# A block of attention and feed-forward layers: another order of TensorE's work, a third value buffer, and the last stage's probability blocks in the k blocks' buffer

## The chip, the cores and the metric

One NeuronCore of a Trainium2 chip. Times are device microseconds of one execution of the program; smaller is better. TensorE (PE) multiplies matrices, VectorE (DVE), ScalarE (ACT) and GpSimd (POOL) work on elements, and SyncE (SP) starts transfers. Each runs its own list of instructions in order and waits on semaphores. SBUF is the memory next to the engines; PSUM, in banks, takes TensorE's results.

## The reference, cut to what matters

x has 32 sequences of 32 positions and 512 channels. Attention has 32 heads of 16.

```python
def attn(x, wq, wk, wv, wo):                 # x here is cond(x): a 32x32 matrix for each sequence
    q, k, v = proj(wq), proj(wk), proj(wv)   # [B, head, T, 16]
    q, k = rope(q), rope(k)
    scores = where(causal, q @ k.T / 4, -inf)
    return (softmax(scores) @ v).merge_heads() @ wo.T

def cond2(x):                                # a linear layer, and LoRA experts, two of eight per token
    gates = top2_softmax(x @ Wr.T + 5 * onehot(language))
    return x @ W.T + 2 * einsum(x @ A, gates, B)

x = x + attn(cond(x, weights[subject]), ...)
x = x + unperm(gelu(perm(cond2(x)) @ up) @ down)    # 16 small feed-forward blocks
```

## The kernel before

The 1024 tokens are 8 tiles of 128; two tiles (t = 0, 1) make a stage's group, and the stages are g = 0 to G-1 = 3. Products of fp32 weights are three matmuls of a high and a low fp32r part (`mm3`); ScalarE writes the high part of every operand (`cond_hi`, `o_out`, `x1_out`) and VectorE the low part (`cond_lo`, `o_lo`, `x1_lo`).

The order of each engine's work is written out by hand in a loop over g. In stage g TensorE does, interleaved: the scores of group g; the feed-forward of group g-1 (`lora_down`, `experts_base`, `turn_logits`, `turn_gates`, `experts_lora`, `ffn_up`, `ffn_down`); the projections of group g+1 (`qk`, `v`); the products of probabilities and values of group g (`pv(g, t, c)`, four chunks c for a tile); and last the output projection `wo_proj(g)`, which needs the high and low parts of both tiles' outputs. `cond` of group g+1 stands at the head of stage g (for g = 1, 2). After the loop comes the feed-forward of group 3 alone, and the scattered output.

The probabilities' way in a stage: `max_shift` (VectorE, from PSUM: maximum and difference) -> `exp` (ScalarE) -> `sums` (VectorE: sum and reciprocal) -> `norm` (GpSimd) -> `turn` (VectorE: transposes of 32x32) -> `probs_block(g, t, i)` (ScalarE): four copies of 32 partitions x 512 that put each sequence's probabilities in its place of the block-diagonal buffer `pbd[:, i]`, the rest of which is zero. `pbd` has two halves i and serves both tiles, so a tile's copy waits for the products that read the half before. k too is laid out in blocks (`kbd`, `k_blocks` on VectorE and GpSimd, after `rope`). `v_out` (ScalarE) copies the values into `vz[:, t]`, one buffer for each tile of a group, when the last group's products of that tile are done; it stands ahead of `o_out` for the same tile. `attn` is the same memory as `xc`, which `cond_hi` and `cond_lo` fill.

PSUM's banks are three rings: A (2 banks: cond, q, k, v; in the last stage pv too), S (2: scores, `ffn_down`) and F (4: pv, `wo_proj`, the rest). The n-th item of a ring takes bank n modulo its size and waits until the item before it in that bank has been read.

The gates of the experts are a chain of small operations on VectorE (`gates_top`, `gate_exp` on ScalarE, `gates_out`, then `turn_gates` on TensorE and `gate_h`), and `experts_lora` waits for it. ScalarE then changes its table (`gelu_table`), copies `x2_out`, and does eight `gelu`s in two halves, each between `ffn_up` and `ffn_down`.

Lines of the page: L504 to L506 are `mm3`, L531 `cond`, L569 and L578 scores, L596 `pv`, L676 `ffn_up`, L688 `ffn_down`, L802 all plain copies of ScalarE, L884 `gelu`, L1005 low parts from PSUM, L1068 and L433 k blocks, L1088 and L1090 `sums`, L1096 `turn`, L418 and L422 GpSimd's part of `rope`, L391 and L479 the memsets of `pbd`, L394 and L401 gathers, L1183 the gathers' indices `idx`, L1030 `blocks`, from which `cond` of group 0 takes its matrices, L1120 and L1140 the logits' copy and the first step of `gates_top`, L1167 the last of `gates_out`, L1176 a cast in `gate_h`, L853 `gelu_table`.

## Time and profile before

| | |
|---|---|
| median of 3 runs | 252.77 us (252.18 to 253.22) |
| the profiled execution: its time, its span | 251.96 us, 250.2 us |
| busy: TensorE, VectorE, ScalarE, GpSimd | 205.5, 147.8, 119.0, 120.0 us |
| mean granted clock of TensorE | 0.952 of full speed |
| stages 0, 1, 2 (start of the stage's work on TensorE) | 39.7, 72.3, 123.9 us |
| stage 3, its `wo_proj` | 175.2, 212.7 us |
| last product of TensorE ends | 239.4 us |

The span runs from the first to the last instruction of the profiled execution; its own time is a little longer. "Busy" is time in which the engine worked; a wait is shown as idle time ahead of an instruction, with the instruction that ended it. The granted clock is 1.0 at 2.4 GHz and 0.5 at 1.2 GHz.

### The profile page before, as it was taken

The numbers are of one execution on the slowest core, as the hardware profiler recorded it, in microseconds if no ns is written. First come the engines' busy times: TensorE is split into PE (matmuls) and PEld (weight loads), VectorE is DVE, ScalarE is ACT, GpSimd is POOL, SyncE is SP. The second block draws the span as 40 slices with busy tenths as digits, with TensorE's granted clock in tenths as the row PEclk, the third lists the DMA queues.
The fourth block names the chain that finished last, engine by engine and source line by source line (L and its number), as shares of the span: only waits on it lengthen the run. The fifth ranks groups of instructions, "written<-read, shape, count | busy, mean of one in ns | idle before, by whom it ended". The sixth has DMA issues, their size and how long they took to land.

```text
span 250.2 us, 5702 instructions
## 1 busy us (share of the span) xinstructions
PE 205.5 (82%) x2404; PEld 176.3 (70%) x2404; DVE 147.8 (59%) x309; ACT 119.0 (48%) x199; POOL 120.0 (48%) x94
## 2 busy tenths in 40 slices
PE   0579997999699999995999999949994828987910
PEld 0579956997598999674988997739883615976500
DVE  3547999968757979681377794832688402235000
ACT  3271537744232238793161379651515995133720
POOL 8258959788700059698200396983003322500054
PEclk9999999999999999998899999998998895999995
DMA  7799823000013000003341000024200003320024
GB/s 235 213 358 344 282 64 107 3 0 3 1 48 125 0 3 3 3 3 42 42 128 45 3 0 0 3 27 59 88 3 0 1 0 45 45 84 0 3 25 59
DMA packets 11273, 15.60 MB, mean 62 GB/s; under 512 B 2320, under 2 KB 7088, under 8 KB 11248
## 3 DMA queue, kind: packets, MB, share of 16 engines
q1 hardware_dynamic: 8224, 11.65, 14.0%
q0 software_dynamic: 2736, 3.57, 9.3%
q8 instruction: 19, 0.31, 0.5%
q10 hardware_dynamic: 288, 0.01, 0.1%
q14 instruction: 6, 0.05, 0.1%
HBM read 10.91 MB, written 4.33 MB: 61 GB/s over the span
## 4 chain that ended last, share of the span: by engine, by line
PE 60%; DVE 14%; ACT 12%; issue 7%; POOL 2%; DMA 2%; POOLq 1%; ACTq 0%; DVEq 0%
PE ps_F L504 8%; PE ps_A L504 8%; PE ps_F L506 7%; PE ps_F L505 7%; PE ps_A L506 7%; PE ps_A L505 7%; ACT pbd L802 7%; PE ps_F L596 3%; PE ps_F L676 3%; PE ps_A L531 3%; PE ps_S L578 2%; ACT act L884 2%; POOL out L453 2%; ACT xc L802 2%; DVE xc L1005 2%
## 5 line engine op out<-in xcount | busy, mean ns | idle before, releaser
L461 POOL TENSOR_TENSOR pr<-pr,small 128x512 f32<-128x512 f32 x16 | 16.5, 1046 | 66.3 <-DVE small L1090 66.3
L802 ACT ACTIVATE pbd<-pr 32x512 f32<-32x512 f32 x64 | 40.2, 628 | 9.8 <-DVE pr L1096 5.0
L453 POOL DMA_INDIRECT out<-y,row_at x16 | 25.1, 1571 | 39.8 <-ACT y L802 36.1
L504 PE MATMUL ps_F<-xc,woT 128*128 128x256 f32 x64 | 19.7, 307 | 6.1 <-DVE xc L1005 6.1
L433 POOL TENSOR_TENSOR kbd<-kr,cst 128x512 f32<-128x512 f32 x16 | 20.7, 1318 | 2.7 <-PE ps_F L513 2.6
L418 POOL TENSOR_TENSOR rot<-rot,cst 128x512 f32<-128x512 f32 x14 | 18.1, 1292 | 7.7 <-DVE rot L1046 7.7
L1068 DVE TENSOR_TENSOR kbd<-kr,cst 128x512 f32<-128x512 f32 x16 | 19.9, 1280 | 2.4 <-POOL kr L422 2.4
L504 PE MATMUL ps_A<-xc,wqT 128*128 128x256 f32 x64 | 18.9, 296 | 2.7 <-DVE xc L1005 2.7
L505 PE MATMUL ps_F<-xc,woT 128*128 128x256 f32 x64 | 19.2, 300 | 0.0
L506 PE MATMUL ps_F<-xc,woT 128*128 128x256 f32 x64 | 19.1, 299 | 0.0
L802 ACT ACTIVATE x<-xt 128x512 fp32r<-128x512 f32 x8 | 5.0, 631 | 28.9 <-DVE xt L1108 28.9
L504 PEld LDWEIGHTS ps_F<-xc,woT 128*128 128x128 f32 x64 | 13.5, 212 | 7.5 <-issue 7.5
L506 PE MATMUL ps_A<-xc,wqT 128*128 128x256 f32 x64 | 18.6, 290 | 0.0
L505 PE MATMUL ps_A<-xc,wqT 128*128 128x256 f32 x64 | 18.5, 289 | 0.0
L504 PE MATMUL ps_A<-xc,wkT 128*128 128x256 f32 x64 | 18.3, 286 | 0.0
L504 PE MATMUL ps_F<-x,w2T 128*128 128x256 f32 x64 | 18.3, 286 | 0.0
L884 ACT ACTIVATE act<-ps_F 128x512 f32<-128x512 f32 x32 | 16.5, 604 | 3.4 <-PE ps_F L676 3.3
L506 PE MATMUL ps_A<-xc,wkT 128*128 128x256 f32 x64 | 17.9, 279 | 0.0
L505 PE MATMUL ps_A<-xc,wkT 128*128 128x256 f32 x64 | 17.9, 279 | 0.0
L506 PE MATMUL ps_F<-x,w2T 128*128 128x256 f32 x64 | 17.8, 279 | 0.0
L505 PE MATMUL ps_F<-x,w2T 128*128 128x256 f32 x64 | 17.8, 279 | 0.0
L531 PE MATMUL ps_A<-wbd,xs 128*128 128x128 f32 x64 | 9.7, 315 | 9.1 <-DVE wbd L1030 9.1
(149 smaller groups left out, 606.0 us busy)
## 6 DMA issues: line engine op xcount, KB each, us to landing
xs<-in_x SPq DMA_DIRECT2D x4, 512.0 KB, 6.4
xt<-in_xT SPq DMA_DIRECT2D x4, 512.0 KB, 3.5
out<-xt SPq DMA_DIRECT2D x4, 512.0 KB, 3.7
pbd<-in_L_attn_wq SPq DMA_DIRECT2D x2, 512.0 KB, 4.7
act<-in_L_attn_wk SPq DMA_DIRECT2D x1, 1024.0 KB, 5.5
act<-in_L_attn_wv SPq DMA_DIRECT2D x1, 1024.0 KB, 8.2
act<-in_L_attn_wo SPq DMA_DIRECT2D x1, 1024.0 KB, 8.2
x<-in_L_cond_A SPq DMA_DIRECT2D x1, 256.0 KB, 9.8
```

The costliest lines, as they stand in the source:

```text
L418: pool.tensor_tensor(rv, rv, con("sin").unsqueeze(1).to_broadcast([P, 2 * N // T, T]), ALU.mult).then_inc(rot_sin, 1)
L433: pool.tensor_tensor(kbd[:, t, c, :, :].rearrange("p b (h s) -> p b h s", h=HG), kv.unsqueeze(2).to_broadcast([P, BT, HG, T]), con("head") ...
L453: pool.indirect_dma_start(out=out, out_offset=bass.IndirectOffsetOnAxis(ap=row_at[:, g, c:c + 1], axis=0), in_=y[:, c, :], in_offset=None, ...
L461: pool.tensor_tensor(pr[:, i, :, :], pr[:, i, :, :], mx[:, i, :].unsqueeze(2).to_broadcast([P, NH // 2, T]), ALU.mult).then_inc(normed, 1)
L504: pe.matmul(dst, hi_l, hi_r, start=start, stop=False, skip_group_check=skip)
L505: pe.matmul(dst, hi_l, lo_r, start=False, stop=False, skip_group_check=skip)
L506: return pe.matmul(dst, lo_l, hi_r, start=False, stop=stop, skip_group_check=skip)
L531: last = pe.matmul(bank(it)[:, P * c:P * c + P], xs[:, g % XS, t, P * c:P * c + P], wbd[:, t, :, :], start=True, stop=True)
L596: last = pe.matmul(bank(it)[32 * j:32 * j + 32, P * c:P * c + P], vz[:, t, 4 * c + j, HD * e:HD * e + 2 * HD], pbd[:, c // 2, HC * (c % 2) ...
L802: return sc.activation(dst, src, ACT.Copy)
L884: sc.activation(act[:, r, j, :, :], bank(it)[:, :].rearrange("p (h n) -> p h n", h=2), ACT.Gelu).then_inc(s_free(it), 1)
L1068: ve.tensor_tensor(kbd[:, t, c, :, :].rearrange("p b (h s) -> p b h s", h=HG), kv.unsqueeze(2).to_broadcast([P, BT, HG, T]), con("head").u ...
```

## The change

1. `cond(g+2)` of stages 0 and 1 stands ahead of `wo_proj(g)`, in place of the head of stage g+1; its copies `cond_hi` and `cond_lo` stand between and behind `x1_out` and `x1_lo`. As `attn` is `xc`, `cond_hi` waits for the whole of `wo_proj`.
2. In stages 1 and 2 tile 0's products come in pairs after each `ffn_up`, and tile 1's around `ffn_down`'s second half.
3. pv moves from the F (and A) ring to the S ring.
4. `vz` has three buffers in turn, and `v_out` waits for the product three tiles back. It now stands ahead of y_out, and `o_out(g, 1)` behind both.
5. In the last stage tile 0's blocks are made before exp 2 and 3 and its products come right behind `turn_gates`; tile 1's blocks go into the two halves of `kbd`, which GpSimd first zeroes (`kbd_zeros`); two of each block's four copies are VectorE's (`probs_half`).
6. The memset of `pbd[:, 1]` on GpSimd stands behind the three first gathers.

```diff
-        vz = sb("vz", [P, GT, NH // 2, 3 * HD])
+        vz = sb("vz", [P, 3, NH // 2, 3 * HD])
+        def pbd_of(g, t, i):
+            return kbd_pbd[i] if (g, t) == (G - 1, 1) else pbd[:, i, :, :, :]
+        def S_at(g):
+            return 8 * g - 2 if g else 0
         def S_scores(g, i):
-            return "S", 4 * g + 2 * max(0, g - 1) + i
+            return "S", S_at(g) + i
+        def PVi(g, t):
+            return "S", S_at(g) + 4 + (2 if g else 1) * t
         def S_down(g, h):
-            return "S", 4 * min(g + 2, G) + 2 * g + h
+            return "S", S_at(g + 1) + (5 + 2 * h if g + 1 < G else h)
...
             pool.memset(vz[:, :, :, :], 0.0).then_inc(vz_zero, 1)
-            pool.memset(pbd[:, 1, :, :, :], 0.0).then_inc(pbd_zero, 1)
...
+            def kbd_zeros(t):
+                wait_full(pool, S_scores(G - 1, 2 * t + 1))
+                pool.memset(kbd[:, t, :, :, :], 0.0).then_inc(kbd_zero, 1)
...
             cond_seqs()
+            pool.memset(pbd[:, 1, :, :, :], 0.0).then_inc(pbd_zero, 1)
```

On TensorE, the head and the middle of stages 1 and 2, and the middle of stage 3:

```diff
-                    if more:
-                        cond(g + 1, 0)
-                        cond(g + 1, 1)
                     scores(g, 0)
...
                 if more:
                     qk(g + 1, "wq", Q, 1)
+                else:
+                    for c in range(KC):
+                        pv(g, 0, c)
...
                     qk(g + 1, "wk", K_, 0)
                     ffn_up(g - 1, 0)
+                    pv(g, 0, 0)
+                    pv(g, 0, 1)
                     qk(g + 1, "wk", K_, 1)
                     ffn_up(g - 1, 1)
+                    pv(g, 0, 2)
+                    pv(g, 0, 3)
+                    v(g + 1, 0)
                     ffn_down(g - 1, 0)
                     ffn_down(g - 1, 1)
-                    v(g + 1, 0)
-                    for c in range(KC):
-                        pv(g, 0, c)
+                    v(g + 1, 1)
+                    pv(g, 1, 0)
+                    pv(g, 1, 1)
                     ffn_down(g - 1, 2)
                     ffn_down(g - 1, 3)
-                    v(g + 1, 1)
-                    for c in range(KC):
-                        pv(g, 1, c)
+                    pv(g, 1, 2)
+                    pv(g, 1, 3)
...
                     ffn_up(g - 1, 0)
-                    pv(g, 0, 0)
-                    pv(g, 0, 1)
                     ffn_up(g - 1, 1)
+                    pv(g, 1, 0)
+                    pv(g, 1, 1)
                     ffn_down(g - 1, 0)
                     ffn_down(g - 1, 1)
-                    pv(g, 0, 2)
-                    pv(g, 0, 3)
-                    for c in range(KC):
-                        pv(g, 1, c)
+                    pv(g, 1, 2)
+                    pv(g, 1, 3)
                     ffn_down(g - 1, 2)
                     ffn_down(g - 1, 3)
+                if g + 2 < G:
+                    cond(g + 2, 0)
+                    cond(g + 2, 1)
                 wo_proj(g, 0)
                 wo_proj(g, 1)
```

ScalarE's and then VectorE's order in stage 3 after the change (several calls to a line here):

```python
exp(g, 0); h_out(g - 1); exp(g, 1); gate_exp(g - 1)
probs_block(g, 0, 0); probs_block(g, 0, 1)
exp(g, 2); exp(g, 3); o_out(g, 0)
gelu_table(g - 1); x2_out(g - 1); gelu(g - 1, 0)
probs_block(g, 1, 0); probs_block(g, 1, 1)
gelu(g - 1, 1); o_out(g, 1); y_out(g - 1, 0); y_out(g - 1, 1)

max_shift(g, 0); max_shift(g, 1); logits_out(g - 1)
sums(g, 0); sums(g, 1); gates_top(g - 1)
turn(g, 0); turn(g, 1); max_shift(g, 2); gates_out(g - 1)
probs_half(0, 0); probs_half(0, 1); max_shift(g, 3); gate_h(g - 1)
sums(g, 2); sums(g, 3); o_lo(g, 0); turn(g, 2); turn(g, 3)
probs_half(1, 0); probs_half(1, 1); o_lo(g, 1)
```

The new helper on VectorE:

```diff
+            def probs_half(t, i):
+                ve.wait_ge(turned, 4 * (G - 1) + 2 * t + i + 1)
+                if t:
+                    ve.wait_ge(kbd_zero, i + 1)
+                else:
+                    wait_pv(ve, 8 * (G - 1) + 2 * i - 3)
+                for b in range(2, BT):
+                    at = slice(T * b, T * b + T)
+                    last = ve.tensor_copy(pbd_of(G - 1, t, i)[at, :, b, :], pT(2 * t + i)[at, :, :])
+                last.then_inc(pbd_v, 1)
```

## Rows read from the trace of the kernel before

**Rows 1.** The page's fourth part: the chain that ended last, by engine.
```profile
PE 60%; DVE 14%; ACT 12%; issue 7%; POOL 2%; DMA 2%; POOLq 1%; ACTq 0%; DVEq 0%
```

**Rows 2.** Stretches of the span: busy time of each engine, granted clock, DMA.
```profile
core 0: us, PE busy (x) PEld busy (x) DVE busy (x) ACT busy (x) POOL busy (x), PEclk, DMA share, GB/s
72.30:74.10 1.80, 1.80 (x19) 1.79 (x18) 0.91 (x2) 0.88 (x2) 0.00 (x0) 1.00 0.00 0
112.40:116.60 4.20, 1.08 (x32) 0.81 (x32) 0.98 (x2) 2.18 (x4) 3.73 (x3) 1.00 0.28 31
116.60:120.00 3.40, 3.34 (x16) 3.37 (x17) 0.00 (x0) 0.00 (x0) 2.79 (x3) 0.51 0.65 70
175.20:187.70 12.50, 12.50 (x210) 10.55 (x208) 9.79 (x31) 4.33 (x7) 0.00 (x0) 1.00 0.14 45
202.00:206.10 4.10, 0.00 (x1) 0.00 (x0) 0.00 (x0) 4.02 (x8) 1.58 (x1) 0.92 0.00 0
206.10:209.20 3.10, 1.93 (x32) 1.51 (x32) 0.69 (x1) 3.04 (x5) 1.56 (x1) 0.50 0.75 84
```

**Rows 3.** TensorE's timeline: start, us, line, operation; [idle before, and who ended it].
```profile
66.57 0.35 PE L504 MATMUL ps_F<-xc,woT 128*128 128x256 f32 x1 [2.02 <-DVE xc L1005]
...
116.66 0.53 PE L504 MATMUL ps_F<-xc,woT 128*128 128x256 f32 x1 [2.02 <-DVE xc L1005]
...
190.91 0.39 PE L504 MATMUL ps_F<-hg,bT 128*128 128x256 f32 x1 [3.16 <-DVE hg L1178]
```

**Rows 4.** GpSimd's and VectorE's timelines at the start, two rows of each.
```profile
2.06 1.80 POOL L391 MEMSET pbd<- 128x2048 f32 x1
...
6.89 1.03 POOL L401 DMA_INDIRECT kr<-in_L_cond_weights,ids  x1 [0.30 <-issue]
...
3.15 0.74 DVE L1183 TENSOR_SCALAR idx<-ids,cst 128x8 uint32<-128x8 int32 x1 [3.15 <-DMA cst<-constants]
...
8.21 0.74 DVE L1030 TENSOR_SCALAR wbd<-wg,cst 128x64 f32<-128x64 f32 x4 [1.03 <-DMA wg<-in_L_cond_weights,idx]
```

**Rows 5.** VectorE, GpSimd and ScalarE at the end of stage 1's attention.
```profile
105.06 1.45 DVE L1068 TENSOR_TENSOR kbd<-kr,cst 128x512 f32<-128x512 f32 x1
...
106.04 1.61 POOL L422 TENSOR_TENSOR kr<-kr,rot 128x512 f32<-128x512 f32 x1
...
114.70 0.60 ACT L802 ACTIVATE vz<-ps_A 128x512 f32<-128x512 f32 x1 [1.20 <-PE ps_F L596]
115.20 0.59 ACT L802 ACTIVATE xc<-ps_F 128x512 fp32r<-128x512 f32 x1
```

**Rows 6.** Groups of stage 3, 175.2 to 212.7: busy us, mean ns, idle before.
```profile
L802 ACT ACTIVATE pbd<-pr 32x512 f32<-32x512 f32 x16 | 10.0, 626 | 0.2
...
L676 PE MATMUL ps_F<-x,upw 32*128 32x256 f32 x32 | 4.6, 522 | 0.0
...
L884 ACT ACTIVATE act<-ps_F 128x512 f32<-128x512 f32 x8 | 4.1, 603 | 0.1
...
L1096 DVE STREAM_TRANSPOSE pr<-pr 128x512 f32<-128x512 f32 x4 | 2.8, 696 | 1.2 <-POOL pr L461 1.2
...
L688 PE MATMUL ps_S<-act,dn 128*32 128x256 f32 x32 | 2.7, 473 | 0.0
...
L1088 DVE TENSOR_REDUCE small<-pr 128x16 f32<-128x512 f32 x4 | 2.6, 656 | 0.0
...
L853 ACT ACT_TABLE_LOAD x1 | 1.3, 1283 | 0.0
...
L1090 DVE RECIPROCAL small<-small 128x16 f32<-128x16 f32 x4 | 1.0, 253 | 0.1
```

**Rows 7.** VectorE's timeline in stage 3, three rows around the gates.
```profile
181.51 0.17 DVE L1140 TENSOR_TENSOR small<-ps_F,small 128x16 f32<-128x16 f32 x1 [1.03 <-PE ps_F L635]
...
186.62 0.29 DVE L1167 TENSOR_SCALAR act<-small 128x256 f32<-128x256 f32 x1
...
189.43 0.96 DVE L1176 CAST hg<-act 128x256 fp32r<-128x256 f32 x1
```

More of the change, by code:

```diff
@@ L149, in ropes_to @@
             return 4 * g + i if g else min(i + 1, 3)
+        kbd_pbd = [kbd[:, i, :, :, :].rearrange("p c b k -> p (c b k)").rearrange("p (h b t) -> p h b t", b=BT, t=T)
+                   for i in range(2)]
+        def pbd_of(g, t, i):
+            return kbd_pbd[i] if (g, t) == (G - 1, 1) else pbd[:, i, :, :, :]
         def pT(i):
@@ L867, in probs_block @@
                     sc.wait_ge(pbd_zero, 2)
-                for b in range(BT):
+                for b in range(BT if g < G - 1 else 2):
                     at = slice(T * b, T * b + T)
-                    last = copy(pbd[at, i, :, b, :], pT(2 * t + i)[at, :, :])
+                    last = copy(pbd_of(g, t, i)[at, :, b, :], pT(2 * t + i)[at, :, :])
                 last.then_inc(pbd_a, 1)
@@ L945, in _ @@
                     gate_exp(g - 1)
-                else:
-                    probs_block(0, 0, 0)
-                    probs_block(0, 0, 1)
+                if g in (0, G - 1):
+                    probs_block(g, 0, 0)
+                    probs_block(g, 0, 1)
                 exp(g, 2)
                 exp(g, 3)
+                if not more:
+                    o_out(g, 0)
                 if g:
@@ L953, in _ @@
                     x2_out(g - 1)
[L954 to L955 removed]
+                if not more:
                     gelu(g - 1, 0)
[L957 removed]
+                    probs_block(g, 1, 0)
+                    probs_block(g, 1, 1)
                     gelu(g - 1, 1)
+                    o_out(g, 1)
                     y_out(g - 1, 0)
[L960 to L963 removed]
                     y_out(g - 1, 1)
[L965 removed]
+                else:
+                    if g:
+                        probs_block(g, 0, 0)
+                        gelu(g - 1, 0)
+                        probs_block(g, 0, 1)
+                        gelu(g - 1, 1)
+                    probs_block(g, 1, 0)
                     v_out(g + 1, 0)
                     o_out(g, 0)
[L968 to L971 removed]
+                    if g:
+                        y_out(g - 1, 0)
+                    probs_block(g, 1, 1)
                     v_out(g + 1, 1)
[L973 to L975 removed]
+                    if g:
+                        y_out(g - 1, 1)
+                    o_out(g, 1)
                 x1_out(g, 0)
+                if g + 2 < G:
+                    wait_full(sc, Fi(g, "WO", 1))
+                    cond_hi(g + 2, 0)
                 x1_out(g, 1)
+                if g + 2 < G:
+                    cond_hi(g + 2, 1)
             h_out(G - 1)
@@ L1221, in _ @@
                 more = g + 1 < G
-                if g:
-                    if more:
-                        cond_lo(g + 1, 0)
-                        cond_lo(g + 1, 1)
-                if g:
+                if g and not more:
+                    max_shift(g, 0)
+                    max_shift(g, 1)
+                    logits_out(g - 1)
+                    sums(g, 0)
+                    sums(g, 1)
+                    gates_top(g - 1)
+                    turn(g, 0)
+                    turn(g, 1)
+                    max_shift(g, 2)
+                    gates_out(g - 1)
+                    probs_half(0, 0)
+                    probs_half(0, 1)
+                    max_shift(g, 3)
+                    gate_h(g - 1)
+                    sums(g, 2)
+                    sums(g, 3)
+                    o_lo(g, 0)
+                elif g:
                     max_shift(g, 0)
@@ L1236, in _ @@
                     sums(g, 1)
-                    if more:
-                        rope(g + 1, 0)
+                    rope(g + 1, 0)
                     turn(g, 0)
@@ L1242, in _ @@
                     sums(g, 3)
-                    if more:
-                        rope(g + 1, 1)
+                    rope(g + 1, 1)
                 else:
@@ L1268, in _ @@
                     w_los("r", raw_r, rT, 1)
-                else:
+                elif more:
                     if g + 2 < G:
                         blocks(g + 2)
-                    if more:
-                        rope(g + 1, 2)
-                    if more:
-                        rope(g + 1, 3)
-                        for t in range(GT):
-                            k_blocks(g + 1, t, 0)
-                            k_blocks(g + 1, t, 2)
+                    rope(g + 1, 2)
+                    rope(g + 1, 3)
+                    k_blocks(g + 1, 0, 0)
+                    k_blocks(g + 1, 0, 2)
                     o_lo(g, 0)
+                    k_blocks(g + 1, 1, 0)
+                    k_blocks(g + 1, 1, 2)
                     o_lo(g, 1)
-                for i in range(2):
-                    add_x(g, i)
-                    x1_lo(g, i)
+                else:
+                    probs_half(1, 0)
+                    probs_half(1, 1)
+                    o_lo(g, 1)
+                add_x(g, 0)
+                x1_lo(g, 0)
+                add_x(g, 1)
+                if g + 2 < G:
+                    cond_lo(g + 2, 0)
+                x1_lo(g, 1)
+                if g + 2 < G:
+                    cond_lo(g + 2, 1)
             logits_out(G - 1)
```

55 lines of the change are left out of this document (22 added, 33 removed).

## The prediction

> **What bounds the kernel now.** I read the chain of waits first: three fifths of it is TensorE, the rest copies of ScalarE and VectorE and waits between engines [rows 1]. So I next cut TensorE's time into stretches, to find where it idles or runs slowly [rows 2], and then asked its timeline who ended each idle time [rows 3]. Four things show.
>
> First, the last copies of the attention output (ScalarE's high part, VectorE's low part) hold TensorE for 2.02 us ahead of `wo_proj` in stages 0 and 1 [rows 3]; stage 2 repeats this. Second, in stage 1 the clock pays as well: from 112.4 to 116.6 TensorE is busy for 1.08 of 4.20 us (the 2.02, and 1.16 for tile 1's last probabilities), and then the granted clock is 0.51, its 1.2 GHz level, until 120.0 [rows 2]. Stage 2 repeats this too. In stage 0 a gap of 2.02 alone stood behind dense work, and its first matmul took 0.35 us, against 0.53 in stage 1 [rows 3]: no fall. Third, `cond`, at the head of stages 1 and 2, takes 1.8 us of a full TensorE [rows 2]. Fourth, stage 3 (175.2 to 212.7, 37.5 us) is TensorE's only to 187.7: it is then held 3.16 us for the gates [rows 3], and afterwards ScalarE is the bound. From 202.0 to 206.1 ScalarE is busy for 4.02 us and TensorE for none, and the clock is 0.50 in the next stretch [rows 2]. ScalarE's largest group there is 16 copies of probabilities, 10.0 us [rows 6].
>
> **Stage 0 to 1: 2.0 us less.** `cond(2)` moves from stage 1's head, where nothing hides it, into the gap ahead of `wo_proj`, and its copies go to the stage's end. That takes 1.8 us off the head. The gap itself shrinks: `v_out` of tile 1 used to wait for the product `pv(g,1,3)` because it overwrote the same `vz`; with a third `vz` it goes ahead, and `o_out` starts 0.50 us sooner (vz at 114.70, xc at 115.20 [rows 5]). The chain of copies becomes 1.5 us, `cond` 1.8, so the longer stands: 2.02 - 1.8 = 0.2. The price is in the copies behind: ScalarE's wait for `wo_proj`'s second half delays only `cond_hi` and `x1_out(g,1)`, which needs that half anyway; VectorE's `x1_lo(g,1)` comes one copy (0.7) later, but `lora_down` needs it only 2.9 us behind the head. `max_shift` comes sooner, as one `cond_lo` no longer stands ahead of `x1_lo`. I cost this at nothing; without its cover it is 0.7 us per stage.
>
> **Stage 1: 4.6 less.** `pv(1,0,.)` moves ahead of `v(2,0)`, so pbd comes free some 8 us sooner, ScalarE fills tile 1's blocks earlier, and the wait of 1.16 goes. `cond(3)` again gives 1.8 + 0.2. Without the idle stretch the clock should stay up: 3.4 us at 0.51 held 1.7 us of work, so 1.6 goes. Against it, TensorE now reaches `turn_logits` just as VectorE has copied the logits: 0.15. Sum: 1.16 + 1.8 + 0.2 + 1.6 - 0.15 = 4.6.
>
> The new orders on the two S banks must not stall it. `pv(1,1,0)` needs the bank that `o_lo(1,0)` reads, and that copy stands on VectorE behind two k blocks, of which the second waits for GpSimd's last rope addition (106.04 + 1.61 [rows 5], 1.9 sooner here, so 105.75). With a k block of 1.45 [rows 5] and a copy of 0.7 the bank is free at 108.0. TensorE began tile 1's products 1.08 ahead of 112.4 [rows 2], so at 111.3; 1.9 sooner, and 1.0 for the `ffn_down` pair that now stands behind them, gives 108.4. The margin is 0.4 us.
>
> **Stage 2: 3.1 less.** As stage 1 without a `cond`: 1.16 + 0.5 + 1.6 - 0.15. One gap of 1.5 stays, as in stage 0, where the clock held.
>
> **Stage 3: 5.3 less (3.4 to 7.2).** Up to the gates' product at 190.9 it gets longer. Ahead of `gate_h` VectorE now has a second sum with reciprocal (0.66 + 0.25 [rows 6], and 0.1 of waiting), two transposes (2 x 0.70 [rows 6]) and `probs_half` for tile 0, four copies of 32x512. Such a copy isn't in this trace. From below: 256 elements in 0.29 and small operations in 0.17 [rows 7] give 0.17 + 2 x 0.12 = 0.42 us; from above 0.70, a transpose. I take 0.4, as it is the same kind of move between two tiles in SBUF, so 1.6 (up to 2.8). Back come VectorE's idle 1.03 ahead of the gates, which the sums fill, and 0.67 of the cast, which took 0.96 beside GpSimd [rows 7]. Net 0.9 + 0.1 + 1.4 + 1.6 - 1.03 - 0.67 = 2.3 later.
>
> The Trainium skill ("VectorE: DVE Perf Modes", Mode 2x_2P) says that a copy with one source and both ends in SBUF moves two fp32 elements a cycle, which would give 0.42 as well; by its plain mode it would be 0.7, and the sum 1.1 worse.
>
> From there to `wo_proj` it took 21.8 us (190.9 to 212.7). Now ScalarE has 8 copies of probabilities fewer, and the four of tile 0 lie in its earlier idle time; tile 1's no longer wait for tile 0's products, as they have their own buffer. Its chain: table load and lookup 1.5 [rows 6], `x2_out` 0.6, `ffn_up` to the first gelu 1.2 (my estimate: over half of a half's 2.3, of which half at the low clock [rows 6]), gelu 2.06 (four at a time overlap a little [rows 6]), four copies 2.5, gelu 2.06, `o_out` 0.6, `y_out` 0.6, `ffn_down` 1.07: 12.3. But TensorE now waits for much of the time around the gates, and with the clock at 1.2 GHz its own chain is longer: one pv pair takes 1.93 in place of 1.08 [rows 2], and `ffn_down`'s two pairs, one at either clock, 2.7 in all [rows 6], so 1.0 and 1.7. Then it is 1.5 + 0.6 + 1.8 + 2.06 + 1.26 = 7.2 up to the first block, 1.9 + 1.7 + 1.9 for pv, ffn_down, pv, then 0.6 + 0.6 + 1.7 and some 0.5 of hand-overs: 16.1. Behind the gates the work is denser, so part of it runs at full clock; I take the middle, 14.2. The stage gives 21.8 - 14.2 - 2.3 = 5.3. The new memsets of kbd (1.80 each, as [rows 4]) lie on GpSimd where it waits for sums.
>
> **The start: 1.0 more.** The memset of pbd's second half moves from ahead of the first gather to behind the third. At 2.06 it held VectorE's 8-column `idx` for 0.74 us, to 0.03 behind the memset's end [rows 4]. Without it the gathers start 0.55 sooner. But then the memset runs from 7.4 to 9.2, and `blocks(0)`, four scalar multiplications that took 0.74 at 8.21, right behind the third gather's end at 7.92 [rows 4], meets it: it ends at 9.95 in place of 8.95, and `cond`, the first product, waits for it. Ends: 0.55 less (no collision) and 1.3 more.
>
> The Trainium skill ("SBUF — State Buffer", Who interferes with whom) says that such one-source operations and GpSimd lock each other out of a shared port pair for a whole instruction, by who comes first; the trace agrees (0.96 for 0.29 [rows 7]), and by the rule the loss is this 1.0.
>
> **Sum.** The profiled execution took 251.96 us with a span of 250.2, 1.76 around it; the median of the runs shown is 0.81 higher, 252.77. Off come 2.0 + 4.6 + 3.1 + 5.3 - 1.0 = 14.0. Span 236.2, its execution 238.0, median 238.8 us. The tail behind `wo_proj(3)`, 37.5, has no edit.
>
> **Rivals.** *The clock is not won.* Idle time of only 1.5 to 1.8 still lets it fall in stages 1 and 2, and stage 3 goes at its slow end: 2 x 1.6 + 1.9 more, 243.9. For it: the fall behind the 4.2 us stretch. Against it: stage 0 holds after 2.02. Chance 0.12.
>
> *Stage 3 gives nothing.* The gates come later still (copies at 0.7, banks waiting for `max_shift(3,3)`), and tile 1 waits for them: stage 3 stays at 37.5, 244.1. For it: TensorE's idle 3.16 for the gates grows to over 5. Chance 0.11.
>
> *All at the good ends*: stage 3 at 7.2, no collision at the start: 238.8 - 1.9 - 1.5 = 235.4. Chance 0.11.
>
> *Slower: the S banks lock.* `o_lo(g,0)` comes late in stages 1 and 2, by the k blocks or by ScalarE. Each microsecond beyond the margin of 0.4 costs one in each stage, and beyond some 3 the clock again (3.2 for both). To lose the whole 14.0 it must be 5.8 us late: 2 x (5.8 - 0.4) + 3.2 = 14.0; at 8 us late the time is 252.8 + 4.4 = 257.2. For it: PV and `ffn_down` now share two banks in strict turn. Against: ScalarE's part ends over 1 us ahead of VectorE's, and that 0.4 ahead of TensorE. Chance 0.03.
>
> *No effect*: stages 0 to 2 are timed by GpSimd's ropes and the gaps only move, 252.8. Against it: GpSimd's chain has the same 1.9 us head start as TensorE's. Chance 0.02.
>
> The forecast has 0.61. Its range is 236 to 242; with the good ends and the first two rivals it is 235.0 to 244.2, each of which has half of its own spread beyond it (0.17 in all), and the last two are left out (0.05). No change means within 0.5%, about what a measurement here can tell: faster 0.95, same 0.02, slower 0.03.
>
> **What would show it.** Right: `cond` between the last pv and `wo_proj` with under 0.3 us idle behind it; a granted clock of 1.00 in `wo_proj` of stages 1 and 2, some 5.7 us long; no 1.16 ahead of pv; in stage 3 the gates' product 18 us behind the head and `wo_proj` 32; VectorE's 32x512 copies at 0.4; `blocks(0)` done at about 9.9. Wrong: an idle time on the S ring ended by VectorE's `xc`, low clock in stages 1 or 2, or a stage 3 near 37.

## The result, and the profile after

The changed kernel takes 241.62 us (median of 4 runs, 240.14 to 244.01) against 252.83 for the kernel before, measured beside it: a ratio of 0.954, 95% interval 0.946 to 0.962; the ratio leaves out one slow execution, the 244.01. The forecast was 238.8. The profiled execution took 240.14 us with a span of 238.3, so 1.84 lies around the span. In two later sets of measurements, on two different chips, the same code gave ratios of 0.948 (0.944 to 0.952) and 0.940 (0.937 to 0.944). That spread turned out to be the main thing to explain.

The page's fourth part of the kernel after, the chain that ended last, by engine, answers to [rows 1]:

```profile
PE 58%; DVE 15%; DMA 9%; POOL 7%; issue 5%; ACT 4%; POOLq 1%; DVEq 0%; ACTq 0%
```

The shares hardly move: TensorE is still most of the chain, ScalarE falls from 12% to 4%, and transfers at the start come in. The stretches show more. These are windows of the kernel after, with the columns of [rows 2]: the end of stage 1's attention, `wo_proj` of stages 1 and 2, and three stretches of stage 3.

```profile
109.00:114.40 5.40, 4.86 (x97) 4.07 (x96) 2.27 (x3) 2.75 (x5) 4.93 (x4) 1.00 0.13 11
114.40:120.20 5.80, 5.71 (x48) 5.72 (x48) 1.38 (x2) 0.63 (x1) 3.88 (x3) 1.00 0.64 75
161.20:167.00 5.80, 5.72 (x48) 5.72 (x48) 1.38 (x2) 0.63 (x1) 4.54 (x3) 1.00 0.62 70
181.60:185.90 4.30, 2.38 (x66) 1.88 (x66) 4.11 (x10) 1.10 (x2) 0.00 (x0) 1.00 0.00 0
185.90:193.40 7.50, 6.64 (x48) 4.85 (x52) 5.19 (x11) 6.61 (x13) 2.06 (x2) 0.84 0.00 0
193.40:200.50 7.10, 5.89 (x97) 3.93 (x96) 0.69 (x1) 3.44 (x7) 0.25 (x1) 0.69 0.01 2
```

The stretch that was 1.08 busy of 4.20 us [rows 2] is now 4.86 of 5.40, and `wo_proj` of stages 1 and 2 is dense at a granted clock of 1.00. The clock is low only in stage 3, from about 191 to 197.8. TensorE's timeline at `wo_proj` of stages 1 and 2 and at the gates' product answers to [rows 3]:

```profile
114.49 0.36 PE L525 MATMUL ps_F<-xc,woT 128*128 128x256 f32 x1 [0.62 <-DVE xc L1040]
...
161.28 0.36 PE L525 MATMUL ps_F<-xc,woT 128*128 128x256 f32 x1 [1.95 <-DVE xc L1040]
...
185.94 0.38 PE L525 MATMUL ps_F<-hg,bT 128*128 128x256 f32 x1 [1.40 <-DVE hg L1225]
```

The 2.02 of stage 0 is gone, that of stage 1 is 0.62, and stage 2 keeps 1.95. In ScalarE's timeline at the end of stage 1 a wait shows that was not forecast:

```profile
111.08 0.60 ACT L830 ACTIVATE y<-ps_S 128x512 f32<-128x512 f32 x1 [0.48 <-PE ps_S L711]
113.02 0.60 ACT L830 ACTIVATE xc<-ps_S 128x512 fp32r<-128x512 f32 x1 [1.35 <-PE ps_S L619]
```

The second row is `o_out(1,1)`. It waits for the last pv, whose rows end at 111.89 (110.83 + 1.06), and starts 1.13 us after that. In stage 2 it starts 0.48 after, in stage 0 0.13. At the start, VectorE and GpSimd (compare [rows 4]):

```profile
3.21 0.23 DVE L1230 TENSOR_SCALAR idx<-ids,cst 128x8 uint32<-128x8 int32 x1 [3.21 <-DMA ids<-in_ids]
8.95 1.42 DVE L1065 TENSOR_SCALAR wbd<-wg,cst 128x64 f32<-128x64 f32 x4 [1.42 <-DMA wg<-in_L_cond_weights,idx]
```

```profile
6.45 1.82 POOL L412 DMA_INDIRECT kr<-in_L_cond_weights,ids  x1 [0.30 <-issue]
8.27 1.82 POOL L486 MEMSET pbd<- 128x2048 f32 x1
```

`idx` is no longer held (0.23), the gathers start 0.44 sooner, but wg is there only at 8.95, and `blocks(0)` runs beside the memset: 1.42 for 0.74. Groups of stage 3 (167.0 to 200.5), to set beside [rows 6]:

```profile
L830 ACT ACTIVATE pbd<-pr 32x512 f32<-32x512 f32 x4 | 2.5, 630 | 0.5 <-DVE pr L1131 0.4
L830 ACT ACTIVATE kbd<-pr 32x512 f32<-32x512 f32 x4 | 2.5, 624 | 0.0
...
L1142 DVE COPY pbd<-pr 32x512 f32<-32x512 f32 x4 | 1.7, 421 | 0.1
...
L1142 DVE COPY kbd<-pr 32x512 f32<-32x512 f32 x4 | 1.7, 421 | 0.1
```

ScalarE's 10.0 us of copies are now 5.0, and VectorE's cost 0.42 each, as forecast. A stage is counted here from its first scores, so that the `cond` that stood at the head of stages 1 and 2 falls to the stage ahead of it. Counted so, the change from before to after is +0.5 up to group 1's first product (42.60 to 43.09), then -2.05, -3.94, -2.74 and -4.0 for stages 0 to 3, and +0.3 in the tail: -11.9 in the span for a forecast of -14.0.

### The profile page after: what moved, and what is told of

It reads as the page before. It is cut to its first block, busy times and chain, and to the rows that moved or that the text cites. A ratio compares the mean times of both kernels' runs of the same rounds, so it can differ in the third digit from the quotient of the medians.

```text
span 238.3 us, 5717 instructions
## 1 busy us (share of the span) xinstructions
PE 199.9 (84%) x2404; PEld 171.7 (72%) x2404; DVE 150.7 (63%) x317; ACT 114.3 (48%) x191; POOL 125.9 (53%) x96
## 4 chain that ended last, share of the span: by engine, by line
PE 58%; DVE 15%; DMA 9%; POOL 7%; issue 5%; ACT 4%; POOLq 1%; DVEq 0%; ACTq 0%
PE ps_F L525 7%; PE ps_A L525 7%; PE ps_F L527 7%; PE ps_F L526 6%; PE ps_S L619 6%; PE ps_A L527 6%; PE ps_A L526 6%; PE ps_F L699 5%; DMA kbd<-in_w2b,permc 4%; PE ps_S L711 3%; DMA act<-in_L_attn_wk 2%; PE ps_S L599 2%; DVE small L1115 2%; POOL out L469 2%; DVE pr L1117 2%
## 5 line engine op out<-in xcount | busy, mean ns | idle before, releaser
L830 ACT ACTIVATE pbd<-pr 32x512 f32<-32x512 f32 x52 | 32.7, 629 | 6.2 <-DVE pr L1131 5.5
L429 POOL TENSOR_TENSOR rot<-rot,cst 128x512 f32<-128x512 f32 x14 | 19.1, 1363 | 7.5 <-DVE rot L1081 7.4
L525 PE MATMUL ps_A<-xc,wqT 128*128 128x256 f32 x64 | 18.1, 283 | 2.8 <-DVE xc L1040 2.8
L525 PE MATMUL ps_F<-xc,woT 128*128 128x256 f32 x64 | 18.2, 285 | 2.6 <-DVE xc L1040 2.6
L527 PE MATMUL ps_F<-xc,woT 128*128 128x256 f32 x64 | 17.9, 279 | 0.0
L526 PE MATMUL ps_F<-x,w2T 128*128 128x256 f32 x64 | 17.9, 279 | 0.0
L526 PE MATMUL ps_F<-xc,woT 128*128 128x256 f32 x64 | 17.9, 279 | 0.0
L527 PE MATMUL ps_F<-x,w2T 128*128 128x256 f32 x64 | 17.9, 279 | 0.0
L526 PE MATMUL ps_A<-xc,wqT 128*128 128x256 f32 x64 | 17.8, 278 | 0.0
L527 PE MATMUL ps_A<-xc,wqT 128*128 128x256 f32 x64 | 17.8, 278 | 0.0
L872 ACT ACTIVATE pr<-pr 128x512 f32<-128x512 f32 x16 | 10.0, 630 | 15.1 <-DVE pr L1117 15.0
L552 PEld LDWEIGHTS ps_A<-wbd,xs 128*128 128x128 f32 x64 | 9.0, 221 | 11.0 <-issue 10.9
```

Source lines behind the costliest of these rows:

```text
L429: pool.tensor_tensor(rv, rv, con("sin").unsqueeze(1).to_broadcast([P, 2 * N // T, T]), ALU.mult).then_inc(rot_sin, 1)
L525: pe.matmul(dst, hi_l, hi_r, start=start, stop=False, skip_group_check=skip)
L526: pe.matmul(dst, hi_l, lo_r, start=False, stop=False, skip_group_check=skip)
L527: return pe.matmul(dst, lo_l, hi_r, start=False, stop=stop, skip_group_check=skip)
L552: last = pe.matmul(bank(it)[:, P * c:P * c + P], xs[:, g % XS, t, P * c:P * c + P], wbd[:, t, :, :], start=True, stop=True)
L830: return sc.activation(dst, src, ACT.Copy)
```

## The experiments

They ran in three sets, each on one chip with the kernel before beside it. Lengths of a stage below are those of the profiled execution, from the first matmul behind one `wo_proj` to the first behind the next; for stage 3 to `wo_proj(3)` itself.

### First set: the new kernel again, the memset, stage 3 undone

**The new kernel, unchanged.** No edit.

> The new kernel unchanged, for its spread and for where its clock falls in another execution. Theory: the 4 us between its runs (240.1 to 244.0) are the granted clock of stages with idle time, above all the last attention stage, so a longer execution has a lower clock there and the other stages stay within 0.3 us. Rival: the longer executions lose their time in data transfers at the start, up to the first product of group 1 (43.1), at the same clock. Also: the copy of the attention output that started 1.13 us behind the last product in stage 1 does so again if a queue holds it, and not if it was chance.

240.25 us median of 6 (239.01 to 243.67), ratio 0.948. The profiled execution (span 239.4) has stage 1 at 47.69 us, as the first one had to the hundredth, but stage 2 at 49.04 in place of 46.79. Its windows around the gap ahead of `wo_proj(2)`:

```profile
158.60:161.00 2.40, 0.03 (x4) 0.00 (x0) 0.69 (x1) 0.60 (x1) 2.09 (x2) 1.00 0.30 23
161.00:164.80 3.80, 3.75 (x19) 3.78 (x20) 0.00 (x0) 0.00 (x0) 3.19 (x3) 0.55 0.67 73
164.80:168.30 3.50, 3.50 (x32) 3.47 (x30) 1.38 (x2) 0.63 (x1) 0.59 (x1) 1.00 0.46 55
```

TensorE idles 2.42 us, since `o_out(2,1)` starts 0.95 behind pv in place of 0.48, and then the clock is at 1.2 GHz for nearly all of 3.8 us (0.55). So the theory holds as to the clock, but the place is stage 2 and not stage 3. In stage 1 the 1.13 came again.

**The memset ahead of the gathers again, and the memset behind `blocks(0)`.**

```
 pool.memset(vz[:, :, :, :], 0.0).then_inc(vz_zero, 1)
+pool.memset(pbd[:, 1, :, :, :], 0.0).then_inc(pbd_zero, 1)   # memset_first
...
 cond_seqs()
+pool.wait_ge(wbd_ready, 1)                                    # memset_late
 pool.memset(pbd[:, 1, :, :, :], 0.0).then_inc(pbd_zero, 1)    # (gone in memset_first)
```

> The memset of pbd's second half ahead of the gathers again, all else new. Theory (the memset's meeting with blocks(0) costs up to 1 us): idx is held to about 4.6, the gathers start 0.7 later than before the change, wg lands at 8.9 to 9.6, blocks(0) takes 0.74 again in place of 1.42 and cond starts at 9.8 to 10.5 in place of 10.51; the kernel is 0.0 to 0.5 us faster. Rival (the gathers' start sets the start): cond starts 0.5 or more later than 10.51 and the kernel is 0.5 us slower.

> The same memset waits for blocks(0). Theory: blocks(0) takes 0.74 us in place of 1.42, cond starts at 9.8 in place of 10.51, and some of the 0.7 us (the last change of 1.4 arrived at stage 0's end as 0.5) is gained: 0.2 to 0.7 us. Rival (wg's landing and the weights' copies bind): blocks(0) is shorter, but the first product of group 1 stays at 43.1 and the time is the same.

With the memset first `idx` ended at 4.52, wg landed at 8.81, `blocks(0)` took 0.74 and `cond` began at 9.70. With it late, `blocks(0)` ran from 8.27 to 9.01, 0.74 us, and `cond` began at 9.16. In the six other profiles of this set and the next the blocks took 1.09 to 2.21 and `cond` began at 9.53 to 10.54. So the collision is real. In all eleven profiles with the memset right behind the gathers, `blocks(0)` ends 0.27 to 0.28 us behind the memset's end, wherever that is; and it moves, as the third gather ahead of it takes 0.87 to 1.88 us of GpSimd. But the whole kernel took 240.93 (ratio 0.952, 0.948 to 0.957) and 241.97 (0.956, 0.952 to 0.959), against 0.948 (0.944 to 0.952) for the new kernel: nothing gained. Both rivals were nearer on the total.

A second effect at the start is as large, and it shows in the kernel before as in some of the later ones. The first products behind `cond`, in TensorE's timeline of the later kernel with all copies on ScalarE:

```profile
15.74 0.55 PE L525 MATMUL ps_A<-xc,wqT 128*128 128x256 f32 x1 [1.46 <-DVE xc L1038]
16.09 0.42 PE L526 MATMUL ps_A<-xc,wqT 128*128 128x256 f32 x1
16.31 0.41 PE L527 MATMUL ps_A<-xc,wqT 128*128 128x256 f32 x1
```

and in the new kernel of the third set:

```profile
15.50 0.36 PE L525 MATMUL ps_A<-xc,wqT 128*128 128x256 f32 x1 [1.46 <-DVE xc L1040]
15.69 0.28 PE L526 MATMUL ps_A<-xc,wqT 128*128 128x256 f32 x1
15.80 0.28 PE L527 MATMUL ps_A<-xc,wqT 128*128 128x256 f32 x1
```

In the first, the matmuls come 0.21 us apart for 3.8 us (2.9 to 3.8 in the five profiles that have it), in the second 0.11 to 0.12 nearly from the start. The granted clock is given as 1.00 in both. But 0.21 is also what the same kind of matmul has in `wo_proj(1)` of the kernel before, where the clock was 0.51 [rows 2]; its timeline there:

```profile
116.99 0.41 PE L505 MATMUL ps_F<-xc,woT 128*128 128x256 f32 x1
117.20 0.42 PE L506 MATMUL ps_F<-xc,woT 128*128 128x256 f32 x1
```

And the first `cond`, just ahead, has its matmuls mostly 0.21 us apart in all fourteen profiles, against 0.11 for the one in stage 0's gap. By their spacing the start of every execution goes at the 1.2 GHz level, and the two forms differ in how long that lasts. The kernel before had the slow form in its profile (wq's first 48 products took 7.41 us), the kernel after the fast one (5.89), 1.5 us less. Compare like with like: in the slow form, `cond` at 9.10 (before) and 9.16 (late memset) led to group 1's first product at 42.60 and 42.72, and at 10.44 to 10.54 (three of the later kernels) to 43.74 to 44.25. So the later `cond` is worth 1.0 to 1.7 us there, not the 0.5 that the profiles of before and after show. In the fast form it does not come out as clearly: `cond` at 9.70 (memset first) led to 43.03, and at 10.18 (the new kernel beside it) to 42.17, so something else sets this point too, and what it is was not found.

**Stage 3 as before the change.** PV results in ring A, tile 1's blocks in pbd, all orders of stage 3 those of before; the core of the edit:

```
+            if g == G - 1:
+                return A(G, t)
             return "S", S_at(g) + 4 + (2 if g else 1) * t
...
-            return kbd_pbd[i] if (g, t) == (G - 1, 1) else pbd[:, i, :, :, :]
+            return pbd[:, i, :, :, :]
...
-                    for c in range(KC):
-                        pv(g, 0, c)
...
                     ffn_up(g - 1, 0)
+                    pv(g, 0, 0)
+                    pv(g, 0, 1)
                     ffn_up(g - 1, 1)
```

> The last attention stage as before the change: its orders on all engines, tile 1's probabilities in pbd, the PV results in ring A, no shared copies; all else new. Theory (the stage's gain of 4.0 is its own orders, buffer and shared copies): the stage takes 37 to 38 us from head to wo_proj in place of 33.5, and the kernel is 4 us slower than the new one, 245.6. Rival (the stage is shorter because it is entered with the work of cond gone and a full clock): it stays under 35.5 us and the kernel is under 243.6.

244.84 us (0.967, 0.963 to 0.970), 4.6 above the new kernel, and the stage took 36.99 us. The rival is out. Its idle times are those of before but for one (1.38 in place of 0.74, ahead of the first product of probabilities); TensorE's timeline:

```profile
183.85 0.38 PE L525 MATMUL ps_F<-hg,bT 128*128 128x256 f32 x1 [3.17 <-DVE hg L1221]
188.68 1.08 PE L617 MATMUL ps_A<-pbd,vz 128*32 128x128 f32 x32 [1.38 <-ACT pbd L827]
193.25 1.08 PE L617 MATMUL ps_A<-pbd,vz 128*32 128x128 f32 x32 [0.44 <-ACT pbd L827]
198.49 1.94 PE L617 MATMUL ps_A<-pbd,vz 128*32 128x128 f32 x32 [4.16 <-ACT pbd L827]
201.58 1.93 PE L617 MATMUL ps_A<-pbd,vz 128*32 128x128 f32 x32 [1.16 <-ACT pbd L827]
```

The 4.16 and 1.16 for tile 1's blocks are what the new order removes. The low clock behind them it does not remove: in the new kernel the clock falls too, only at another place.

### Second set: one part of the change at a time

**All copies on ScalarE in stage 3.** VectorE's `probs_half` and TensorE's wait for it go, ScalarE copies four rows of blocks as elsewhere.

```
-                for b in range(BT if g < G - 1 else 2):
+                for b in range(BT):
...
-                    probs_half(0, 0)
-                    probs_half(0, 1)
...
-                    probs_half(1, 0)
-                    probs_half(1, 1)
```

> In the last attention stage ScalarE makes all four copies of each block again and VectorE none; the buffer and the orders are the new ones. Theory (the stage's tail is ScalarE's chain, and the shared copies take 4 x 0.63 off it behind the gates, while VectorE's four ahead of the gates cost 1.7): the gates' product comes 1.0 to 1.7 us sooner than 18.9 behind the head, the rest is 2.0 to 2.5 longer than 14.6, so the stage takes 34 to 35 us in place of 33.5 to 34.9 and the kernel is 0.5 to 1.0 us slower (241 to 242). Rival (the separate buffer and the order of pv did it all, the copies beside VectorE only moved the work): the kernel is the same or faster, 239 to 240.

239.36 us (ratio 0.943, 0.936 to 0.950), stage 3 33.18 us against 33.51 and 33.35 in the two executions of the new kernel so far. The forecast loss did not come, and the time is the rival's. That sharing gives nothing is not shown by this: no unchanged kernel ran in this set, and the clock was low at two places of this stage, in the other two executions at one. TensorE's timeline shows what took the place of the old waits:

```profile
187.74 1.53 PE L697 MATMUL ps_F<-x,upw 32*128 32x256 f32 x16 [0.32 <-ACT x L828]
189.63 2.50 PE L697 MATMUL ps_F<-x,upw 32*128 32x256 f32 x16 [0.37 <-ACT act L912]
193.49 1.83 PE L617 MATMUL ps_S<-kbd,vz 128*32 128x128 f32 x32 [1.35 <-ACT kbd L828]
```

The gates' product began 17.9 us behind the head in place of 18.9, and what that gave went into 1.35 us of waiting for tile 1's blocks.

**`cond` at the head of the stage.** On all three engines it stands at the head of stages 1 and 2 again:

```
                 if g:
+                    if more:
+                        cond(g + 1, 0)
+                        cond(g + 1, 1)
                     scores(g, 0)
...
-                if g + 2 < G:
-                    cond(g + 2, 0)
-                    cond(g + 2, 1)
                 wo_proj(g, 0)
```

> cond, cond_hi and cond_lo at the head of stages 1 and 2 again, the third vz and all else new. Theory: each of the two heads gets 1.8 us longer and the gap ahead of wo_proj opens again to 2.0 (stage 0) and 2.4 (stage 1), so 1.8 per stage, 3.6 in all, and the clock falls now and then in wo_proj of stage 1 as it did in some executions of stage 2 (1.6 more): 244 to 246. Rival (the copies behind cond, moved to the stage's end, cost what cond at the head cost): 241 to 242.

242.56 us (0.956, 0.948 to 0.964), 3.2 more than the kernel just above, whose code is the new one up to stage 3; the two intervals still touch, and the stages say more. Stages 1 and 2 took 48.11 and 48.33 us against 46.63 and 46.69 there: 1.5 and 1.6 for `cond`. The gap came back, ahead of `wo_proj(1)`:

```profile
115.85 0.35 PE L525 MATMUL ps_F<-xc,woT 128*128 128x256 f32 x1 [1.59 <-DVE xc L1038]
```

It is 1.59 us long, and the clock stayed at 1.00 in both stages. So what `cond` in the gap saved here is its own length; the clock held without it.

**The output copied ahead of y's second half.**

```
-                    if g:
-                        y_out(g - 1, 1)
                     o_out(g, 1)
+                    if g:
+                        y_out(g - 1, 1)
```

> In stages 1 and 2 ScalarE copies the attention output of tile 1 ahead of y's second half. Behind y's copy it started 1.1 us (stage 1) and 0.95 us (stage 2) after the last product, in stages 0 and 3, with no y copy just ahead, 0.1. Theory (something on ScalarE behind the y copy holds it): it starts within 0.1 to 0.2 us of the last product, wo_proj(1) then waits only for cond (no idle, 0.6 less) and the gap in stage 2 is 1.5, with the clock at 1.00: 1.5 to 3 us faster. Rival (TensorE's last pv ends later than modelled, or its signal comes late, when ffn_down stands between the pv pairs): the copy starts 1.0 late again and nothing changes.

237.38 us (0.937, 0.927 to 0.946). The copy starts 0.12 and 0.13 behind the last pv. But that is no proof: in the two kernels above, which keep y's copy ahead of it, it also starts 0.12 and 0.13 behind. Stages 1 and 2 are 46.63 and 46.68 us, the same as in the kernel with all copies on ScalarE. What it has over that one comes from `cond` at 9.53 in place of 10.53, the fast form of wq's products, and stage 3 (32.56 us), none of which the edit touches.

**The old order of pv in stages 1 and 2.** TensorE's order of before from `ffn_up` to pv, the S ring renumbered for it, ScalarE's and VectorE's orders to match:

```
                     qk(g + 1, "wk", K_, 0)
                     ffn_up(g - 1, 0)
-                    pv(g, 0, 0)
-                    pv(g, 0, 1)
                     qk(g + 1, "wk", K_, 1)
                     ffn_up(g - 1, 1)
...
                     v(g + 1, 1)
+                    for c in range(KC):
+                        pv(g, 1, c)
...
+            if 0 < g < G - 1:
+                return "S", S_at(g) + 5 + 2 * t
```

> In stages 1 and 2 the old order of pv, ffn_down and v (pv of a tile in one run, tile 1's last), ScalarE's and VectorE's orders to match; cond at the end and the third vz stay. Theory: TensorE waits 1.16 us again for tile 1's last probabilities in both stages; the gap ahead of wo_proj in stage 2 is 1.5 (no late start of the copy), and the 1.16 + 1.5 behind each other let the clock fall in stage 2, in stage 1 too only if cond does not fill it: 1.2 + 1.2 + 1.6 less 0.9 = 2 to 4 us slower, 242.5 to 244.5. Rival (the new order of pv only moved the wait to the late o_out): 240 to 241.

240.37 us (0.950, 0.942 to 0.957), stages 1 and 2 48.12 and 47.70: 1.5 and 1.0 longer. TensorE's timeline:

```profile
158.78 2.06 PE L623 MATMUL ps_S<-pbd,vz 128*32 128x128 f32 x64 [1.19 <-DVE xc L1042]
162.43 0.36 PE L529 MATMUL ps_F<-xc,woT 128*128 128x256 f32 x1 [1.59 <-DVE xc L1042]
```

The wait is not for the probabilities, as before the change, but for the S bank that `o_lo(2,0)` reads behind the k blocks, because PV shares that ring here. The size is right for another reason than the expected one. Two gaps of 1.19 and 1.59, with 2.1 us of products between them, left the clock at 1.00; gaps of 1.16 and 2.02 with 1.08 between them had not [rows 2]. What the new order of pv is worth by itself stays open, since the old order was not tried with PV in the F ring.

What was unforeseen is stage 3. Its code is that of the new kernel, but it took 31.07 us in place of 33.51. What tells the two apart in the windows is the clock, the last column but two:

```profile
183.00:187.00 4.00, 3.13 (x66) 2.62 (x65) 3.82 (x9) 1.10 (x2) 0.00 (x0) 0.66 0.00 0
187.00:193.00 6.00, 5.27 (x42) 4.07 (x43) 5.02 (x11) 5.14 (x11) 2.06 (x2) 0.94 0.00 0
193.00:199.00 6.00, 4.47 (x106) 3.01 (x98) 0.69 (x1) 4.92 (x9) 0.24 (x1) 1.00 0.01 3
```

The clock fell once, some 16 us behind the head, while TensorE waits for the gates anyway, and not again. In the first profile of the new kernel it was at 1.00 there and fell at 24 us behind the head, when `ffn_up`, pv and `ffn_down` follow each other with ScalarE waiting for them.

### Third set: what is late, and what is left

**The new kernel once more.**

> The new kernel unchanged once more, on the same chip as the next three. The copy of tile 1's attention output started 1.1 us (stage 1) and 0.95 us (stage 2) late in four executions of one chip, and 0.12 in four of another, among them a kernel whose code is the same up to stage 3. Theory (it hangs on the chip or the execution, not on the order of instructions): here both stages show the same kind of value, either near 1 or near 0.12, whatever kernel runs. Rival (it hangs on the kernel): again 1.1 and 0.95 here, and 0.12 in the kernel with o_out ahead of y's second half. Time 239 to 241.5.

237.35 us (0.940, 0.937 to 0.944), 2.9 under the first set, though the kernel before was 252.87 and 253.41 in the two. ScalarE's timeline at the end of stage 1:

```profile
110.99 0.60 ACT L830 ACTIVATE y<-ps_S 128x512 f32<-128x512 f32 x1 [0.48 <-PE ps_S L711]
111.92 0.60 ACT L830 ACTIVATE xc<-ps_S 128x512 fp32r<-128x512 f32 x1 [0.34 <-PE ps_S L619]
```

The same two copies, the same 0.48 ahead of the first; the second waits 0.34 instead of 1.35. So the late start hangs on the chip or the set, not on the order: 0.12 or 0.13 in stages 1 and 2 of all eight profiles of the second and third sets, 0.95 to 1.14 in all of the four of the first, and 1.13 and 0.48 in the first profile of all. With it prompt, stage 1 takes 46.62 us and stage 2 46.68, at a clock of 1.00, and stage 3 goes as in the kernel just above, in 31.65, with the clock low once and early. Windows of stage 3:

```profile
180.70:184.80 4.10, 3.62 (x67) 3.15 (x65) 3.91 (x10) 0.63 (x1) 0.00 (x0) 0.59 0.00 0
184.80:190.00 5.20, 3.67 (x34) 2.87 (x31) 4.86 (x11) 4.25 (x8) 2.06 (x2) 0.99 0.00 0
190.00:197.40 7.40, 5.87 (x112) 3.98 (x111) 0.83 (x2) 6.27 (x12) 0.27 (x1) 1.00 0.01 2
```

**Only tile 1's copies shared; y's first half early in stage 3; all three edits together.**

```
-                for b in range(BT if g < G - 1 else 2):
+                for b in range(2 if (g, t) == (G - 1, 1) else BT):   # split_tile1, best
...
-                    probs_half(0, 0)
-                    probs_half(0, 1)
...
                     gelu(g - 1, 1)
+                    y_out(g - 1, 0)                                   # y_early, best
                     o_out(g, 1)
-                    y_out(g - 1, 0)
```

> In the last attention stage ScalarE alone copies tile 0's probabilities, the two engines share tile 1's. All four on ScalarE took TensorE's 0.5 and 1.4 us of waiting ahead of the gates' product away, but made it wait 1.35 us for tile 1's blocks. Theory (VectorE's copies of tile 0 stand ahead of the gates, ScalarE is idle there; behind the gates it is the reverse): neither wait is there, the gates' product starts 17.9 behind the head in place of 18.9, the stage is 1.0 to 1.3 us shorter, the kernel 238.5 to 239.5. Rival (TensorE's clock falls instead, its slow stretch only comes at another place): the stage is within 0.4 us of 33.5 and the kernel the same.

> In the last attention stage ScalarE copies y's first half ahead of the attention output of tile 1. Its last ffn_down waited 1.21 us for that bank, with ScalarE idle 2.6 us before it. Theory: the wait goes, the copy of the output still starts right behind the last pv, and wo_proj then waits for VectorE's low part (0.6 + 0.7 + hand-overs, 1.5 behind pv) in place of 2.2: 0.7 us faster, whichever clock. Rival (y's copy delays the output's): the same time.

> The three together: o_out ahead of y's second half in stages 1 and 2, only tile 1's copies shared, y's first half ahead of o_out in stage 3. Theory (they act at different places): 0 to 1.5 us of o_out, 1.0 of the copies, 0.7 of y: 236.5 to 238.5, 1.5 to 3 us under the new kernel on the same chip. Rival (the time is set by where TensorE's clock falls, which moves by 1 to 2.4 us between executions): 239 to 241, intervals overlapping with the new kernel's.

Medians 237.28, 237.28 and 237.01 us, ratios 0.938, 0.940 and 0.938, each interval overlapping with the 0.937 to 0.944 of the unchanged kernel beside them: no difference that can be told, so none of the gains that were forecast over the new kernel is confirmed. The profiles show what became of each. With tile 1's copies alone shared, neither wait is there, and the gates' product comes 18.03 behind the head, as expected; but the stage took 32.20 us, with the clock low a second time, at pv of tile 1 (1.62 and 1.46 us for 1.08). With y early (TensorE's timeline):

```profile
195.54 1.07 PE L711 MATMUL ps_S<-act,dn 128*32 128x256 f32 x16 [0.85 <-ACT y L830]
196.85 0.35 PE L525 MATMUL ps_F<-xc,woT 128*128 128x256 f32 x1 [0.24 <-DVE xc L1040]
```

Of the 1.34 that this `ffn_down` waits in the unchanged kernel beside it, 0.85 is left: at full clock ScalarE was at its gelu until 194.99 and came to y only then, so the idle time on which the expectation rested belonged to the execution with the low clock. The stage took 31.27, the three together 30.98, against 31.65. `best` is the fastest by its median, by 0.3 us, which is not beyond chance.

## Why the prediction was right, point by point

**The whole.** 14.0 less was forecast; 11.2 was measured at first, 13.2 and 15.5 in the later sets. The direction and, but for the sharing of copies below, the mechanisms held; two of the sizes, the hand-over behind the last pv and the place where the clock falls in stage 3, vary with the same code, and no row of the kernel before could give them. The 2.8 us between 238.8 and 241.62 are 0.7 too much hoped for in stage 1, 0.4 in stage 2, 1.3 in stage 3, 0.3 in the tail, less 0.5 at the start (each rounded); the last 0.7 is that the median lies 1.48 above the profiled execution, for 0.81 before.

**`cond` into the gap: right.** Stage 0 gave 2.05 for 2.0, with no idle time ahead of `wo_proj`. Undone, it cost 1.5 and 1.6 us in the two stages and 3.2 in the whole, for a forecast of 2.0 per stage; with the third vz and the new place of `v_out` the gap was already down from 2.02 to 1.59. The copies moved to the end of the stage cost nothing that shows.

**Stage 1: 4.6 forecast, 3.94 measured, 5.0 where the copy is prompt** (46.63 against 51.63 before). The pv order, the S banks (`pv(1,1,0)` does not stall) and the clock came as described, though it is not shown which part holds the clock: with `cond` back at the head, and with the old order of pv, it stayed at 1.00 as well. The term that was mis-sized is the hand-over from the last pv to `o_out`: 0.1 in the sum, 1.13 in this profile. Of this, 0.88 reaches `wo_proj` (2.68 us behind the first matmul of `cond`, against 1.80 where the copy is prompt). The rest of the 1.06 between the stages (47.69 against 46.63) is 0.2 in `wo_proj` itself, 5.89 us for 5.69; two of the late profiles have 5.69 and 5.68 there.

**Stage 2: 3.1 forecast, 2.74 measured, 2.85 where the copy is prompt.** The gap is 1.5 as forecast there (1.59 in the trace), 1.95 in the first profile, 2.42 to 2.45 in the four of the first set, of which three had the clock fall behind it, and 49.0 us of stage for 46.7. That was the first rival, weighed at 0.12. It holds for the longer gap alone: no gap of 1.59 or 1.95 was followed by a fall.

**Stage 3: 5.3 forecast (3.4 to 7.2), 4.0 measured, 5.8 in the third set.** Up to the gates' product the forecast was 18.0 behind the head, the trace has 18.9. The 0.9 is one instruction, in VectorE's timeline of the kernel after:

```profile
174.03 0.17 DVE L1191 TENSOR_REDUCE small<-small 128x2 f32<-128x16 f32 x1
174.23 1.07 DVE L1192 TENSOR_TENSOR small<-small 128x16 f32<-128x16 f32 x1
175.34 0.17 DVE L1193 SCALAR_TENSOR_TENSOR small<-small,cst 128x16 f32<-128x16 f32 x1
```

GpSimd multiplies the probabilities from 173.22 to 175.27, because the first two sums now come ahead of the gates, and a step of 0.18 took 1.07. It took 1.06 or 1.07 in all twelve profiles with the new order of stage 3, and in neither of the two with the old one. The sum had moved the sums and left out what they start on GpSimd. Behind the gates 14.58 was measured for 14.2; the middle between two clocks was taken, and the executions fall on either side of it (31.07 to 34.15 us for the same stage). That 14.58 came so near 14.2 is therefore in part luck. (The lower of its two chains adds up to 12.2, not 12.3, and 0.17 + 2 x 0.12 is 0.41; neither moves the result.) Undone, the stage is worth 4.6 us. The sharing of the copies has no gain that shows: their prices (0.42 each) were right, but the four ahead of the gates hold the gates' product back by 1.05 us (18.93 against 17.88 behind the head), and without any sharing the stage took 33.18. Whether the four behind the gates give more than that is open, as the place of the low clock moves the stage by more. The buffer of its own for tile 1 and the order of pv did most of the work (36.99 to 33.18); this is shown for the two together, not for each.

**The start: 1.0 lost was forecast, 0.5 measured, and that by luck.** `blocks(0)` took 1.42 in place of 0.74, and up to 2.21; it ended at 10.37 for a forecast of 9.95, since the gather ahead of the memset took 1.82 and not 1.03. `cond` began 1.4 later, and in the slow form the loss at group 1's first product is 1.0 to 1.7 us. That the first profiles show 0.5 is due to the slow form in the one and the fast form in the other. By the port rule of the Trainium skill ("SBUF — State Buffer", Who interferes with whom) such a one-source operation of VectorE and one of GpSimd shut each other out for a whole instruction. The trace agrees in that `blocks(0)` takes 0.74 in the three kernels where the memset lies elsewhere, and otherwise ends 0.27 to 0.28 behind the memset. That the one issued first has the ports, as the page also says, the rows do not bear out: in three profiles the first of the four operations starts 0.02 to 0.12 us ahead of the memset and is held until its end all the same. The loss did not come back in the total when the memset was moved away; wq's slow or fast form (1.5 us) and the place of the clock's fall (up to 2.4 us) move by more.

**What stays open.** Why `o_out(g,1)` starts a microsecond late on some chips or in some sets, and whether o_out ahead of y would cure it there: it was not tried in a set in which it was late. Why the spacing of 0.21 us at the start lasts into wq's products in some executions. And why the kernel with the late memset was 1.7 us slower than the new one; its profile shows the slow form, the fall in stage 2 and the low clock twice in stage 3, but not that the edit brings them.

## What to carry to other kernels

Work that nothing waits for soon is worth its whole length when it is moved from a dense stretch into a gap that a chain of copies leaves in TensorE; here 1.5 to 2 us per stage. That it also holds up the clock is not shown here. Where two engines take turns around a chain, a copy moved from one to the other can gain only on the side where its old owner is the bound: see for each half of the work which engine is idle at that moment, and what a piece of work that comes sooner starts on a third engine. Before half a microsecond is hunted in one profile, take a second one on another chip: here the same code differed by 2.9 us, more than any of the last three edits could give.

## What the runs showed that was not expected

- The granted clock fell in stage 3 in every profile of the new order, but at a place that moved: at pv of tile 0, where TensorE waits for the gates anyway, the stage took 31.07 to 31.65 us (30.98 and 31.27 with y early); at `ffn_up` and tile 1's pv 33.3 to 33.5; at both 32.2 to 34.2.
- A gap of 2.42 to 2.45 us ahead of `wo_proj(2)` was followed by the 1.2 GHz level at once (two executions), 1.4 us into `wo_proj` (one), or not at all (one). Gaps of 1.59 and 1.95 there never were.
- Matmuls 0.21 us apart in place of 0.12 at the start, the spacing that the 1.2 GHz level has elsewhere in these traces, stood beside a granted clock of 1.00: the column does not show every slow stretch, the matmuls' spacing does.
- ScalarE's copy behind the last pv of stages 1 and 2 started 0.12 or 0.13 us after it in eight profiles and 0.5 to 1.1 in five; four of the eight run the new kernel's code up to stage 3. What delayed it is not known.
